# Differential attention and a gated feed-forward on one core: the second exponentials' scaling moved from two engines to ScalarE alone, with corrected entries in the build-time plan

## The chip, the cores and the metric

The kernel runs on one core of a Trainium2 chip. The metric is the device time of one execution in microseconds (us). The core has five engines that work through their own instruction lists in order and wait on semaphores: TensorE (PE in the profile, PEld for its weight loads), VectorE (DVE), ScalarE (ACT), GpSimd (POOL), and SyncE (SP), which here only issues transfers.

## The reference

The input is 2048 tokens of 256 values. The reference is a differential attention with 16 query heads and 8 key heads of width 128, and then a gated feed-forward, each with a layer norm before and behind it and a residual.

```python
def attn_map(qi, ki):
    s = jnp.einsum('bqhd,bkhd->bhqk', qi, ki) * scale
    s = jnp.where(causal, s, neg)
    return jax.nn.softmax(s, axis=-1)
p1 = attn_map(q[:, :, :, 0], k[:, :, :, 0])
p2 = attn_map(q[:, :, :, 1], k[:, :, :, 1])
lam = lam1 - lam2 + LAMBDA_INIT
p = p1 - lam * p2
o = jnp.einsum('bhqk,bkhe->bqhe', p, v)
rms = jax.lax.rsqrt(jnp.mean(o * o, axis=-1, keepdims=True) + EPS)
o = o * rms * subln_w * (1.0 - LAMBDA_INIT)
return o.reshape(B, S, H * D) @ out_w.T + out_b
...
x = fwht(x * SU_ug) / SCALE
x = jax.nn.silu(x @ W_gate.T * ws_gate) * (x @ W_up.T * ws_up)
x = fwht(x * SU_dp) / SCALE
x = x @ W_down.T * ws_down
```

## The kernel before

**Tiling.** The attention is cut into 4 groups of heads, a group into 16 *duos*, a duo into two blocks of 128 query rows that together see 17 key blocks. A duo `d` has 5 chunks `j` of 128 to 512 keys. So there are 64 duos and 320 chunks. For each chunk the score matrix is made twice, `m = 0` and `m = 1` (640 score chunks).

**One chunk's way.** PE makes the scores in one of four score banks (lines 1038, 1041 and 1044). DVE takes the maximum (1441, with the mask 1436, negated by 1445). ACT takes the exponential and its row sum (step `E`, line 1211), which frees the score bank; `m = 0` goes to a ring named e1, `m = 1` to a ring named e2 (both are called `e_all` in the rows). When both maps of a block are done, DVE works out `ratio` (1733: minus lambda times the one sum over the other) and `gain` (1736). Then e2 is multiplied by `ratio` (step `E2`: by ACT in line 1226 or by POOL in line 1782), POOL adds it to e1 (step `MIX`, line 1749), ACT writes the high half of the product with `gain` as 16-bit numbers (step `SPLIT`, line 1233), DVE the low half (line 1452), SP issues a transposing transfer, and PE multiplies the result by the values (step `PV`, lines 1065 to 1067). The output of a block is then normed (ACT 1241, DVE 1708, POOL 1756, ACT 1249, DVE 1482), transposed and multiplied by the output weights (step `OP`, 1118).

**Around it.** Query projections (step `QP`, PE 1137, ACT 1267, DVE 1494) run two blocks of tokens ahead. In the last group the weights of the feed-forward are prepared between the chunks: POOL builds a Hadamard matrix (`HAD`) and eight sums or differences of weight halves (`FB`, line 1859), ACT and DVE split each (`FH`, 1334 and 1616), PE multiplies by the matrix (`F`), and ACT (1352) and DVE (1624) move the product out of its bank. Of the four weight loads for that, two are issued behind `FB` 1 and 3, and `FB` 4 to 7 read them.

**What sets the order.** `plan()` runs when the kernel is built. It steps through time with a recorded duration for every operation, starts on each engine the ready head with the lowest rank (then the oldest), and so writes out five fixed lists, one for each engine. The hardware then follows these lists; a step whose input is late holds up all that stands behind it in its list. `E` has rank 1, `MIX` and `SPLIT` rank 2, `E2` on ACT rank 3. In `start`, POOL may take a `MIX` whose `E2` nobody has begun, and then does the `E2` itself just ahead of it; an `E2` that POOL has taken is dropped from ACT's line.

Of the kernel before, what the change touches and what calls it, by code (L numbers as in the profile page):

```python
# [173 lines left out]
def plan():  # L174
# [5 lines left out]
    waiting, ending, now, count = {}, [], [0.0], [0]  # L180
    scaling, mixed = set(), set()
    free_at = {e: 0.0 for e in ("PE", "ACT", "DVE", "POOL", "SP")}
# [12 lines left out]
    def spawn(kind, what):  # L195
        pe = ("PE", kind, what)
        if kind == "S":
# [4 lines left out]
            if last:  # L202
                own = [jj for jj, ch in enumerate(duo_chunks(d)) if ch[0] == o]
                for jj in own:
                    qq, ww = CHUNKS * d + jj, duo_chunks(d)[jj][4]
                    room = [("DVE", "SPLIT", duo_of(x)) for x in e1_blockers[qq]] if m == 0 else \
                        [("SP", "SPLIT", duo_of(x)) for x in e2_blockers[qq]]
                    add("E", "ACT", "E", (d, m, jj), 0.23 + 0.00084 * ww, [("DVE", "S", what)] + room, 1)
                if m == 1:
                    add("I", "DVE", "SUMS", o, 0.1, [("ACT", "E", (d, 1, own[-1]))], 0)  # L210
                    add("I", "DVE", "INV", o, 0.08, [("DVE", "SUMS", o)], 0)
                    add("I", "DVE", "GAIN", o, 0.16, [("DVE", "INV", o)] + ([] if o else [("DVE", "LAM2", None)]), 0)
                    for jj in own:
                        qq, ww = CHUNKS * d + jj, duo_chunks(d)[jj][4]
                        room = [("PE", "PV", duo_of(x)) for x in pt_blockers[qq]]
                        add("A", "ACT", "E2", (d, jj), 0.19 + 0.00083 * ww, [("DVE", "GAIN", o)], 3)
                        add("M", "POOL", "MIX", (d, jj), 0.19 + 0.00212 * ww, [("DVE", "GAIN", o)], 2)
                        add("H", "ACT", "SPLIT", (d, jj), 0.19 + 0.00083 * ww, [("POOL", "MIX", (d, jj))], 2)
                        add("L", "DVE", "SPLIT", (d, jj), 0.13 + 0.00115 * ww, [("ACT", "SPLIT", (d, jj))], 2)
                        add("T", "SP", "SPLIT", (d, jj), 0.3 + 0.002 * ww, [("DVE", "SPLIT", (d, jj))] + room, 0, 2.2)  # L220
        elif kind == "PV":
            o, last = duo_chunks(what[0])[what[1]][0], duo_chunks(what[0])[what[1]][5]
            if last:
                add("P", "ACT", "SQ", o, 0.40, [pe] + ([("DVE", "VE", o - 4)] if o >= 4 else []), 0)
                add("N", "DVE", "VE", o, 0.08, [("ACT", "SQ", o)], 0)
                add("N", "POOL", "OT", o, 0.55, [("DVE", "VE", o)] + ([("DVE", "OL", o - 4)] if o >= 4 else []), 0)
                add("R", "ACT", "OH", o, 0.29, [("POOL", "OT", o)] + ([("SP", "OX", o - 4)] if o >= 4 else []), 0)
                add("R", "DVE", "OL", o, 0.4, [("ACT", "OH", o)], 0)
                add("X", "SP", "OX", o, 1.2, [("DVE", "OL", o)] + ([("PE", "OP", o - 4)] if o >= 4 else []), 0, 2.2)
# [266 lines left out]
    def start(engine):  # L496
        for line in (waiting.get(("ACT", "A"), ()),):
            while line and line[0][1].what in mixed:
                line.popleft()
        heads = [line[0] for (e, _), line in waiting.items() if e == engine and line]  # L500
        heads = [(op.rank, n, op) for n, op in heads if all(x in done for x in op.after)
                 and not (op.kind == "MIX" and op.what in scaling and ("ACT", "E2", op.what) not in done)]
        if not heads:
# [5 lines left out]
        us = op.us  # L509
        if op.kind == "E2":  # L510
            scaling.add(op.what)
# [82 lines left out]
def build(nc, hidden, w_qkv, w_o, cols, rows, lams, w_ug, w_d, out):  # L594
# [10 lines left out]
    with ExitStack() as whole:  # L605
# [18 lines left out]
        with ExitStack() as att:  # L624
# [128 lines left out]
            def h_tile(c, jt, lo, tt):  # L753
# [34 lines left out]
             s_full, s_act, s_dve, t_full, t_hi, t_lo, r_full, r_hi, r_free, kv_full, kv_act, kv_dve, v_lo,  # L788
             neg_ready, sums_ready, ratio_step, ratio_ready, gain_ready, e2_scaled, e2_act, p_pool, p_hi, p_lo, pv_done, o_hi, o_lo,
             msq_ready, rms_step, rms_ready) = semaphores(  # L790
# [83 lines left out]
            def e2_of(q, w):  # L874
                return e2_all[:, e2_places[q]:e2_places[q] + w]
# [320 lines left out]
            def _(act):  # L1196
# [543 lines left out]
            def _(pool):  # L1740
                def mix(d, j):
                    o, s, _, _, w, _ = duo_chunks(d)[j]
                    q = CHUNKS * d + j
                    a, b = e1_of(q, w), e2_of(q, w)
                    if (d, j) in scaled_by_act:
                        pool.wait_ge(e2_act, scaled_by_act[d, j] + 1)
                    else:
                        pool.wait_ge(e2_scaled, scaled_by_pool[d, j] + 1)
                    pool.tensor_tensor(a, a, b, ALU.add).then_inc(p_pool, 1)  # L1749
# [224 lines left out]
```

## Time and profile before

| | |
|---|---|
| median of 3 runs | 1285.94 us (1284.38 to 1286.74) |
| profiled execution, its own time | 1285.75 us |
| its span, first to last instruction | 1283.5 us |
| mean granted TensorE clock | 0.985 |
| busy: PE, DVE, ACT, POOL | 1210.5, 1066.1, 995.4, 700.8 us |
| `E2` on ACT (line 1226) | 197 times, 121.5 us |
| `E2` on POOL (line 1782) | 123 times, 89.6 us |
| `MIX` on POOL (line 1749) | 320 times, 372.9 us |

The attention fills the span from about 60 us to about 1130 us; behind it only the feed-forward runs. Matmuls overlap in the records, so PE's busy time is time in which at least one is under way. Two neighbouring instructions of ACT or DVE overlap a little in the same way.

### The profile page before, as it was taken

Reading aid. Unit: us, or ns where it says so; the run is one execution under the profiler, and the core shown is the slowest. Engines: PE = TensorE matmul, PEld = TensorE weight load, DVE = VectorE, ACT = ScalarE, POOL = GpSimd, SP = SyncE. Lnnn points to the kernel's source line nnn. Section 1 sums busy time; section 2 is a strip of 40 time slices with the busy share of each in tenths; the row PEclk is TensorE's granted clock in tenths of the full one; section 3 lists DMA queues with packets and bytes.
Section 4 is the critical chain, followed back from the end, with each engine's and each line's share of the span. In section 5 each row is a group of like instructions: output and inputs, shape, how many; then the busy total and the mean of one; then the engine's idle time right before and its main releaser. Section 6 shows DMA issues by size and latency. Waiting matters only on the chain.

```text
span 1283.5 us, 26516 instructions
## 1 busy us (share of the span) xinstructions
PE 1210.5 (94%) x8102; PEld 1018.7 (79%) x8102; DVE 1066.1 (83%) x2876; ACT 995.4 (78%) x2599; POOL 700.8 (55%) x797
## 2 busy tenths in 40 slices
PE   8899999999999999999999999999988797898998
PEld 7787887877888878888878788788876685786887
DVE  6889999888789998989799989888889899637545
ACT  5788888889688888978789889887877788745341
POOL 3464645454655655536565655445588574556532
PEclk9899999999999999999999999999998899999999
DMA  3145545564265554532555455445543453720001
GB/s 128 57 76 105 88 85 89 102 101 71 50 127 90 99 91 89 103 70 55 126 97 95 85 94 102 74 75 114 100 85 76 93 90 69 143 46 1 29 17 37
DMA packets 368154, 106.62 MB, mean 83 GB/s; under 512 B 359312, under 2 KB 365712, under 8 KB 367504
## 3 DMA queue, kind: packets, MB, share of 16 engines
q1 hardware_dynamic: 366672, 103.37, 42.6%
q8 instruction: 67, 1.10, 0.4%
q10 hardware_dynamic: 1344, 1.57, 0.3%
q14 instruction: 71, 0.58, 0.1%
HBM read 14.71 MB, written 2.10 MB: 13 GB/s over the span
## 4 chain that ended last, share of the span: by engine, by line
PE 47%; DVE 29%; issue 8%; ACT 8%; POOL 4%; DMA 4%; SPq 1%; ACTq 0%; DVEq 0%; POOLq 0%
DVE p L1452 7%; PE score_bank L1172 7%; DVE mx L1441 6%; PE score_bank L1038 5%; PE score_bank L1044 4%; PE score_bank L1041 4%; ACT e_all L1211 4%; DVE score_bank L1436 4%; PE turn_bank L1065 2%; POOL e_all L1749 2%; PE turn_bank L1066 2%; PE turn_bank L1067 2%; DMA p16T<-p 2%; PE proj_bank L1065 2%; PE proj_bank L1067 2%
## 5 line engine op out<-in xcount | busy, mean ns | idle before, releaser
L1749 POOL TENSOR_TENSOR e_all<-e_all 128x512 f32<-128x512 f32 (+3 forms) x320 | 372.9, 1179 | 141.9 <-ACT e_all L1226 131.6
L1211 ACT ACTIVATE e_all<-score_bank,negmx 128x512 f32<-128x512 f32 (+2 forms) x640 | 394.1, 625 | 60.8 <-DVE negmx L1445 46.3
L1038 PE MATMUL score_bank<-k_hi,q_hi 128*128 128x512 f32 (+2 forms) x640 | 257.1, 402 | 32.9 <-ACT e_all L1211 16.9
L1452 DVE SCALAR_TENSOR_TENSOR p<-e_all,gain,p 128x512 f16<-128x512 f32 (+3 forms) x320 | 266.2, 846 | 9.3 <-ACT p L1233 8.9
L1441 DVE TENSOR_REDUCE mx<-score_bank 128x1 f32<-128x512 f32 (+1 forms) x384 | 242.5, 636 | 18.3 <-PE score_bank L1044 17.4
L1041 PE MATMUL score_bank<-k_lo,q_hi 128*128 128x512 f32 (+2 forms) x640 | 233.0, 364 | 0.4 <-DVE k_lo L1502 0.4
L1044 PE MATMUL score_bank<-k_hi,q_lo 128*128 128x512 f32 (+2 forms) x640 | 233.1, 364 | 0.0
L1233 ACT ACTIVATE p<-e_all,gain 128x512 f16<-128x512 f32 (+3 forms) x320 | 203.9, 665 | 13.0 <-POOL e_all L1749 12.6
L1038 PEld LDWEIGHTS score_bank<-k_hi,q_hi 128*128 128x128 f32 x640 | 121.7, 190 | 75.6 <-ACT e_all L1211 33.6
L1782 POOL TENSOR_SCALAR e_all<-e_all,ratio 128x512 f32<-128x512 f32 (+3 forms) x123 | 89.6, 728 | 156.8 <-DVE ratio L1733 155.9
L1756 POOL TENSOR_TENSOR few<-few,half_neg 128x1 f32<-128x1 f32 x128 | 78.5, 614 | 142.0 <-DVE few L1708 141.8
L1065 PE MATMUL turn_bank<-v,p16T 128*128 128x256 f16 x553 | 152.4, 276 | 3.7 <-DVE q_lo L1494 1.7
L1066 PE MATMUL turn_bank<-v,p16T 128*128 128x256 f16 x553 | 151.6, 274 | 0.0
L1067 PE MATMUL turn_bank<-v,p16T 128*128 128x256 f16 x553 | 151.5, 274 | 0.0
L1226 ACT ACTIVATE e_all<-e_all,ratio 128x512 f32<-128x512 f32 (+2 forms) x197 | 121.5, 660 | 16.5 <-DVE ratio L1733 16.3
L1044 PEld LDWEIGHTS score_bank<-k_hi,q_lo 128*128 128x128 f32 x640 | 121.5, 190 | 14.0
L1211 ACT ACTIVATION_READ_ACCUMULATOR e_all<-score_bank,negmx 128x1 f32 x640 | 131.9, 206 | 0.0
L1041 PEld LDWEIGHTS score_bank<-k_lo,q_hi 128*128 128x128 f32 x640 | 122.3, 191 | 7.0 <-DVE k_lo L1502 0.6
L1436 DVE CUSTOM_DVE_ANT_0 score_bank<-score_bank,mask 128x384 f32<-128x384 f32 (+2 forms) x192 | 110.7, 577 | 14.7 <-PE score_bank L1044 14.3
L1065 PE MATMUL proj_bank<-v,p16T 128*128 128x256 f16 x326 | 89.4, 274 | 0.0
L1067 PE MATMUL proj_bank<-v,p16T 128*128 128x256 f16 x326 | 89.0, 273 | 0.0
L1066 PE MATMUL proj_bank<-v,p16T 128*128 128x256 f16 x326 | 89.0, 273 | 0.0
(393 smaller groups left out, 2738.6 us busy)
## 6 DMA issues: line engine op xcount, KB each, us to landing
p16T<-p SPq DMA_TRANSPOSE x320, 3.1
w_raw<-in_w_qkv_dram SPq DMA_DIRECT2D x3, 1024.0 KB, 5.3
w_raw<-in_w_o_dram SPq DMA_DIRECT2D x4, 512.0 KB, 3.3
oT<-o SPq DMA_TRANSPOSE x128, 2.5
bv<-in_hidden_dram SPq DMA_DIRECT2D x8, 256.0 KB, 2.9
w_raw<-in_w_ug_dram SPq DMA_DIRECT2D x4, 512.0 KB, 4.3
out_dram<-e SPq DMA_DIRECT2D x16, 128.0 KB, 1.7
e<-in_w_d_dram SPq DMA_DIRECT2D x1, 1024.0 KB, 5.9
```

The costliest lines, as they stand in the source:

```text
L1038: pe.matmul(bank[:, 0:w], qh, kh, start=True, stop=False)
L1041: pe.matmul(bank[:, 0:w], qh, kl, start=False, stop=False)
L1044: pe.matmul(bank[:, 0:w], ql, kh, start=False, stop=True).then_inc(s_full, 1)
L1065: pe.matmul(bank[:, 0:HID], hi, v16[:, kt, 0, :], start=(kt == 0), stop=False)
L1066: pe.matmul(bank[:, 0:HID], hi, v16[:, kt, 1, :], start=False, stop=False)
L1067: mm = pe.matmul(bank[:, 0:HID], lo, v16[:, kt, 0, :], start=False, stop=(kt == i))
L1211: act.activation(e, S[k % NS][:, 0:w], ACT.Exp, bias=negmx[:, d % 2, m, s:s + 1], scale=-1.0 if alone else 1.0, accum_out=ssum[:, d % 4, s ...
L1233: act.activation(halves_of(q, w)[0], e1_of(q, w), ACT.Copy, scale=gain[:, d % 4, s:s + 1]).then_inc(p_hi, 1)
L1436: dve.tensor_tensor_reduce(out=S[k % NS][:, 0:w], in0=S[k % NS][:, 0:w], in1=mask[:, BANK - w:], scale=1.0, scalar=LOWEST, op0=ALU.add, op ...
L1441: dve.tensor_reduce(mx[:, d % 2, m, s, c:c + 1], S[k % NS][:, 0:w], X, ALU.max)\
L1452: dve.scalar_tensor_tensor(out=halves_of(q, w)[1], in0=e1_of(q, w), scalar=gain[:, d % 4, s:s + 1], in1=halves_of(q, w)[0], op0=ALU.mult, ...
L1749: pool.tensor_tensor(a, a, b, ALU.add).then_inc(p_pool, 1)
```

## The change

All 320 `E2` are ACT's, with rank 2 instead of 3; in the plan a `MIX` waits for its `E2`; POOL's form of it, and the two sets by which the engines shared them, are gone. POOL's wait is now for ACT's count of `E2`, which are done in the order of the chunks. Some recorded durations of the plan are changed: `GAIN` 0.16 to 0.26, DVE's `SPLIT` 0.00115 to 0.00104 a column, `SQ` 0.40 to 0.37, `VE` 0.08 to 0.13, `OH` 0.29 to 0.37. The plan also learns that the two late weight loads take 5.0 and that `FB` 4 to 7 wait for them. No instruction but `E2` changes its engine or its form.

```diff
-                    add("I", "DVE", "GAIN", o, 0.16, [("DVE", "INV", o)] + ([] if o else [("DVE", "LAM2", None)]), 0)
+                    add("I", "DVE", "GAIN", o, 0.26, [("DVE", "INV", o)] + ([] if o else [("DVE", "LAM2", None)]), 0)
...
-                        add("A", "ACT", "E2", (d, jj), 0.19 + 0.00083 * ww, [("DVE", "GAIN", o)], 3)
-                        add("M", "POOL", "MIX", (d, jj), 0.19 + 0.00212 * ww, [("DVE", "GAIN", o)], 2)
+                        add("A", "ACT", "E2", (d, jj), 0.19 + 0.00083 * ww, [("DVE", "GAIN", o)], 2)
+                        add("M", "POOL", "MIX", (d, jj), 0.19 + 0.00212 * ww, [("ACT", "E2", (d, jj))], 2)
...
-                        add("L", "DVE", "SPLIT", (d, jj), 0.13 + 0.00115 * ww, [("ACT", "SPLIT", (d, jj))], 2)
+                        add("L", "DVE", "SPLIT", (d, jj), 0.13 + 0.00104 * ww, [("ACT", "SPLIT", (d, jj))], 2)
...
-            add("FB", "POOL", kind, what, 1.35, [("POOL", "HAD", None)] + ([("DVE", "FH", what - 2)] if what > 1 else []), 3)
-            add("D", "SP", kind, what, 0.3, [("POOL", kind, what)], 1)
+            loaded = [("SP", "FB", what // 2 * 2 - 3)] if what >= 4 else []
+            add("FB", "POOL", kind, what, 1.35, [("POOL", "HAD", None)] + ([("DVE", "FH", what - 2)] if what > 1 else []) + loaded, 3)
+            add("D", "SP", kind, what, 0.3, [("POOL", kind, what)], 1, 5.0 if what in (1, 3) else 0.0)
...
-        if op.kind == "MIX":
-            mixed.add(op.what)
-            if op.what not in scaling:
-                orders[engine].insert(-1, ("E2", op.what))
-                us += 0.32 + 0.00085 * duo_chunks(op.what[0])[op.what[1]][4]
...
-                        act.activation(e, e, ACT.Copy, scale=ratio[:, d % 4, s:s + 1]).then_inc(e2_act, 1)
+                        act.activation(e, e, ACT.Copy, scale=ratio[:, d % 4, s:s + 1]).then_inc(e2_scaled, 1)
...
-                    if kind == "E2":
-                        d, j = what
-                        o, s, _, _, w, _ = duo_chunks(d)[j]
-                        e = e2_of(CHUNKS * d + j, w)
-                        pool.wait_ge(ratio_ready, o + 1)
-                        pool.tensor_scalar(e, e, ratio[:, d % 4, s:s + 1], 0.0, ALU.mult, ALU.add).then_inc(e2_scaled, 1)
```

The lists that the plan writes differ in many places. Three of them follow. The line numbers of the changed kernel are lower by 14 on DVE and ACT in these parts (1212 is 1226, 1610 is 1624) and by 17 to 23 on POOL (1732 is 1749, 1836 is 1859).

ACT in the second group, around duo 21, in the kernel before:

```order
L1233 ACTIVATE p_78<-e_all,gain 128x512
L1226 ACTIVATE e_all<-e_all,ratio 128x384
L1233 ACTIVATE p_78<-e_all,gain 128x384
L1226 ACTIVATE e_all<-e_all,ratio 128x384
L1211 ACTIVATE e_all,ssum<-score_bank,negmx 128x512
L1211 ACTIVATE e_all,ssum<-score_bank,negmx 128x384 x2
L1233 ACTIVATE p_78<-e_all,gain 128x384 x2
L1211 ACTIVATE e_all,ssum<-score_bank,negmx 128x512
```

and in the changed kernel:

```order
L1219 ACTIVATE p_78<-e_all,gain 128x512
L1212 ACTIVATE e_all<-e_all,ratio 128x512
L1212 ACTIVATE e_all<-e_all,ratio 128x384
L1253 ACTIVATE q_hi<-turn_bank,bq 128x256
L1197 ACTIVATE e_all,ssum<-score_bank,negmx 128x512
L1197 ACTIVATE e_all,ssum<-score_bank,negmx 128x384
L1219 ACTIVATE p_78<-e_all,gain 128x512
L1219 ACTIVATE p_78<-e_all,gain 128x384
L1212 ACTIVATE e_all<-e_all,ratio 128x384
L1197 ACTIVATE e_all,ssum<-score_bank,negmx 128x512
```

Scalings (1212) now stand two in a row here, ahead of the exponentials (1197) and of a query projection (1253).

POOL in the last group, between the sums of weights `FB` 4, 5 and `FB` 6, 7, in the kernel before:

```order
L1859 TENSOR_TENSOR v_sum<-w_raw 128x512 x2
L1782 TENSOR_SCALAR e_all<-e_all,ratio 128x512
L1749 TENSOR_TENSOR e_all<-e_all 128x512 x2
L1782 TENSOR_SCALAR e_all<-e_all,ratio 128x384
L1749 TENSOR_TENSOR e_all<-e_all 128x384
L1782 TENSOR_SCALAR e_all<-e_all,ratio 128x384
L1749 TENSOR_TENSOR e_all<-e_all 128x384
L1782 TENSOR_SCALAR e_all<-e_all,ratio 128x384
L1749 TENSOR_TENSOR e_all<-e_all 128x384
L1782 TENSOR_SCALAR e_all<-e_all,ratio 128x256
L1749 TENSOR_TENSOR e_all<-e_all 128x256
L1782 TENSOR_SCALAR e_all<-e_all,ratio 128x512
```

(two more scalings and three more sums of 512 follow ahead of `FB` 6), and in the changed kernel:

```order
L1836 TENSOR_TENSOR v_sum<-w_raw 128x512 x2
L1732 TENSOR_TENSOR e_all<-e_all 128x384
L1732 TENSOR_TENSOR e_all<-e_all 128x512 x2
L1732 TENSOR_TENSOR e_all<-e_all 128x384 x2
L1836 TENSOR_TENSOR v_sum<-w_raw 128x512 x2
```

The scalings are gone, and five sums (1732) instead of nine stand between the two pairs.

DVE a little later, up to the first of two steps that take the product of the folds `F` 2 and 3 out of its bank (1624), in the kernel before:

```order
L1441 TENSOR_REDUCE mx<-score_bank 128x1
L1452 SCALAR_TENSOR_TENSOR p_78<-e_all,gain,p_78 128x384 x2
L1452 SCALAR_TENSOR_TENSOR p_78<-e_all,gain,p_78 128x256
L1452 SCALAR_TENSOR_TENSOR p_78<-e_all,gain,p_78 128x512 x2
L1718 TENSOR_REDUCE s_97<-ssum 128x2
L1708 TENSOR_SCALAR few<-few 128x1
L1452 SCALAR_TENSOR_TENSOR p_78<-e_all,gain,p_78 128x512
L1723 RECIPROCAL inv<-s_97 128x2
L1624 SCALAR_TENSOR_TENSOR spare<-turn_bank,su_s,spare 128x512
```

and in the changed kernel:

```order
L1427 TENSOR_REDUCE mx<-score_bank 128x1
L1438 SCALAR_TENSOR_TENSOR p_78<-e_all,gain,p_78 128x384
L1438 SCALAR_TENSOR_TENSOR p_78<-e_all,gain,p_78 128x256
L1468 SCALAR_TENSOR_TENSOR o_64<-turn_bank,few,o_64 128x256
L1704 TENSOR_REDUCE s_97<-ssum 128x2
L1709 RECIPROCAL inv<-s_97 128x2
L1719 SCALAR_TENSOR_TENSOR ratio<-s_97,inv,neg_lam 128x1
L1722 TENSOR_SCALAR gain<-inv,few 128x1
L1438 SCALAR_TENSOR_TENSOR p_78<-e_all,gain,p_78 128x512
L1610 SCALAR_TENSOR_TENSOR spare<-sum_bank,su_s,spare 128x512
```

Three low halves (1438) instead of six stand between the last maximum and that step.

## Rows read from the trace of the kernel before

**Rows 1.** The page: busy time by engine; the chain that ended last, by engine
```profile
PE 1210.5 (94%) x8102; PEld 1018.7 (79%) x8102; DVE 1066.1 (83%) x2876; ACT 995.4 (78%) x2599; POOL 700.8 (55%) x797
...
PE 47%; DVE 29%; issue 8%; ACT 8%; POOL 4%; DMA 4%; SPq 1%; ACTq 0%; DVEq 0%; POOLq 0%
```

**Rows 2.** Busy time by stretch: PE, PEld, DVE, ACT, POOL; granted clock, DMA share
```profile
60.00:1080.00 1020.00, 971.12 (x6772) 818.74 (x6771) 906.53 (x2466) 865.21 (x2319) 583.40 (x647) 0.99 0.49 90
840.00:1080.00 240.00, 214.28 (x1466) 180.64 (x1464) 212.84 (x572) 197.80 (x523) 156.10 (x182) 0.96 0.46 89
```

**Rows 3.** The first of these stretches, POOL's line 1782 alone
```profile
60.00:1080.00 1020.00, 84.86 (x117) 0.99 0.49 90
```

**Rows 4.** Groups by form, ACT's line 1226: busy us, mean ns, idle before
```profile
L1226 ACT ACTIVATE e_all<-e_all,ratio 128x512 f32<-128x512 f32 x98 | 67.5, 721 | 13.2 <-DVE ratio L1733 13.1
...
L1226 ACT ACTIVATE e_all<-e_all,ratio 128x384 f32<-128x384 f32 x89 | 52.0, 614 | 3.0 <-DVE ratio L1733 2.9
...
L1226 ACT ACTIVATE e_all<-e_all,ratio 128x256 f32<-128x256 f32 x7 | 3.5, 503 | 0.3 <-DVE ratio L1733 0.2
```

**Rows 5.** Groups by form, POOL's line 1782
```profile
L1782 POOL TENSOR_SCALAR e_all<-e_all,ratio 128x512 f32<-128x512 f32 x62 | 48.0, 774 | 100.2 <-DVE ratio L1733 99.6
...
L1782 POOL TENSOR_SCALAR e_all<-e_all,ratio 128x384 f32<-128x384 f32 x47 | 33.7, 716 | 39.7 <-DVE ratio L1733 39.5
```

**Rows 6.** The waits: who waited for whom, us in total, times, longest
```profile
POOL e_all L1782 <- DVE ratio L1733: 155.9, 65, 10.2
...
POOL e_all L1749 <- ACT e_all L1226: 131.6, 52, 10.2
...
PEld score_bank L1038 <- ACT e_all L1211: 33.6, 60, 2.9
...
ACT o L1249 <- POOL few L1756: 26.3, 39, 3.8
...
ACT p L1233 <- POOL e_all L1749: 12.6, 27, 1.0
```

**Rows 7.** Busy time in a slice of 16 us
```profile
512.00:528.00 16.00, 15.97 (x120) 13.81 (x119) 15.68 (x39) 15.78 (x43) 9.91 (x12) 1.00 0.42 95
```

**Rows 8.** The same slice, POOL's line 1782 alone
```profile
512.00:528.00 16.00, 1.69 (x3) 1.00 0.42 95
```

**Rows 9.** POOL's timeline near 378 us: start, duration
```profile
377.74 0.69 POOL L1782 TENSOR_SCALAR e_all<-e_all,ratio 128x512 f32<-128x512 f32 x1
```

**Rows 10.** DVE's timeline at the same moment
```profile
377.98 0.99 DVE L1452 SCALAR_TENSOR_TENSOR p<-e_all,gain,p 128x512 f16<-128x512 f32 x1 [0.97 <-ACT p L1233]
```

**Rows 11.** DVE's line 1452: duration min/median/max in ns, all forms
```profile
L1452 DVE SCALAR_TENSOR_TENSOR p<-e_all,gain,p x320: 342/741/1829, 60.0 to 1124.0; 128x512 f16<-128x512 f32 x80, 128x384 f16<-128x384 f32 x68, 128x256 f16<-128x256 f32 x8, 128x128 f16<-128x128 f32 x4
```

**Rows 12.** PE's timeline at 1002 us, with the idle time before it
```profile
1002.36 0.80 PE L1137 MATMUL turn_bank<-xT_hi,wq_hi 128*128 128x256 f32 x2 [6.89 <-DVE spare L1624]
```

**Rows 13.** DVE's timeline from 995 to 1002 us
```profile
995.39 5.35 DVE L1452 SCALAR_TENSOR_TENSOR p<-e_all,gain,p 128x384 f16<-128x384 f32 x5
...
1001.59 0.72 DVE L1624 SCALAR_TENSOR_TENSOR spare<-turn_bank,su_s,spare 128x512 fp32r<-128x512 f32 x1
```

**Rows 14.** The slice around it: busy time and granted clock
```profile
992.00:1008.00 16.00, 9.11 (x48) 7.53 (x46) 14.58 (x29) 7.99 (x20) 11.55 (x13) 0.68 0.28 54
```

**Rows 15.** The chain at and behind it: start, us, what
```profile
1002.36 1.65 PE turn_bank L1137 x6
...
1007.66 0.21 PE proj_bank L1067
1007.88 0.11 PE proj_bank L1065
...
1011.72 0.71 PE turn_bank L1137 x6
```

**Rows 16.** POOL's line 1859 (the folds' sums), and its engine's idle time before it
```profile
L1859 POOL TENSOR_TENSOR v_sum<-w_raw x8: 1264/1294/1829, 950.7 to 997.6; 128x512 f32<-128x512 f32 x8
its engine sat idle before it (us, times) until:
```

More of the change, by code:

```diff
@@ L180, in plan @@
     waiting, ending, now, count = {}, [], [0.0], [0]
-    scaling, mixed = set(), set()
     free_at = {e: 0.0 for e in ("PE", "ACT", "DVE", "POOL", "SP")}
@@ L223, in spawn @@
             if last:
-                add("P", "ACT", "SQ", o, 0.40, [pe] + ([("DVE", "VE", o - 4)] if o >= 4 else []), 0)
-                add("N", "DVE", "VE", o, 0.08, [("ACT", "SQ", o)], 0)
+                add("P", "ACT", "SQ", o, 0.37, [pe] + ([("DVE", "VE", o - 4)] if o >= 4 else []), 0)
+                add("N", "DVE", "VE", o, 0.13, [("ACT", "SQ", o)], 0)
                 add("N", "POOL", "OT", o, 0.55, [("DVE", "VE", o)] + ([("DVE", "OL", o - 4)] if o >= 4 else []), 0)
-                add("R", "ACT", "OH", o, 0.29, [("POOL", "OT", o)] + ([("SP", "OX", o - 4)] if o >= 4 else []), 0)
+                add("R", "ACT", "OH", o, 0.37, [("POOL", "OT", o)] + ([("SP", "OX", o - 4)] if o >= 4 else []), 0)
                 add("R", "DVE", "OL", o, 0.4, [("ACT", "OH", o)], 0)
@@ L496, in start @@
     def start(engine):
-        for line in (waiting.get(("ACT", "A"), ()),):
-            while line and line[0][1].what in mixed:
-                line.popleft()
         heads = [line[0] for (e, _), line in waiting.items() if e == engine and line]
-        heads = [(op.rank, n, op) for n, op in heads if all(x in done for x in op.after)
-                 and not (op.kind == "MIX" and op.what in scaling and ("ACT", "E2", op.what) not in done)]
+        heads = [(op.rank, n, op) for n, op in heads if all(x in done for x in op.after)]
         if not heads:
@@ L509, in start @@
         us = op.us
-        if op.kind == "E2":
-            scaling.add(op.what)
-        if op.kind == "MIX":
-            mixed.add(op.what)
-            if op.what not in scaling:
-                orders[engine].insert(-1, ("E2", op.what))
-                us += 0.32 + 0.00085 * duo_chunks(op.what[0])[op.what[1]][4]
         free_at[engine] = now[0] + us
@@ L794, in build @@
                 "r_hi", "r_free", "kv_full", "kv_act", "kv_dve", "v_lo", "neg_ready", "sums_ready", "ratio_step",
-                "ratio_ready", "gain_ready", "e2_scaled", "e2_act", "p_pool", "p_hi", "p_lo", "pv_done", "o_hi", "o_lo", "msq_ready",
+                "ratio_ready", "gain_ready", "e2_scaled", "p_pool", "p_hi", "p_lo", "pv_done", "o_hi", "o_lo", "msq_ready",
                 "rms_step", "rms_ready")
@@ L844, in build @@
                             neg_use[o, m] = len(neg_use)
-            scaled_by_act = {x: n for n, x in enumerate([x for k, x in orders["ACT"] if k == "E2"])}
-            scaled_by_pool = {x: n for n, x in enumerate([x for k, x in orders["POOL"] if k == "E2"])}
             WORK = (T[0], T[1], R, O)
@@ L1744, in mix @@
                     a, b = e1_of(q, w), e2_of(q, w)
[L1745 to L1748, printed above, removed]
+                    pool.wait_ge(e2_scaled, q + 1)
                     pool.tensor_tensor(a, a, b, ALU.add).then_inc(p_pool, 1)
@@ L1776, in _ @@
                 for kind, what in orders["POOL"] + tail:
-                    if kind == "E2":
-                        d, j = what
-                        o, s, _, _, w, _ = duo_chunks(d)[j]
-                        e = e2_of(CHUNKS * d + j, w)
-                        pool.wait_ge(ratio_ready, o + 1)
-                        pool.tensor_scalar(e, e, ratio[:, d % 4, s:s + 1], 0.0, ALU.mult, ALU.add).then_inc(e2_scaled, 1)
-                    elif kind == "MIX":
+                    if kind == "MIX":
                         mix(*what)
```

2 lines of the change are left out of this document (1 added, 1 removed).

## The prediction

> **What bounds the kernel now.** I read the page first. PE has work under way for 94% of the span, DVE for 83%, ACT for 78%, POOL for 55%, and the chain that ended last runs 47% over PE, 29% over DVE and only 8% over ACT [rows 1]. The change touches the attention alone, so the busy time by stretch is the next view. From 60 to 1080 us PE is busy 971.1 of 1020 us (95%), DVE 906.5 (89%), ACT 865.2 (84.8%), POOL 583.4 (57%) [rows 2]. Three engines are close to full and feed each other in fixed lists: PE leads, but neither DVE nor ACT has much to give. The last part differs: from 840 to 1080 us PE is at 214.3 of 240 us (89%) and DVE at 212.8 (89%), with the clock at 0.96 [rows 2]. There PE is not the leader; the work on the feed-forward's weights makes DVE and POOL late.
>
> The waits say what an idle moment is worth. POOL waits 155.9 us for `ratio` ahead of its scalings and 131.6 us for ACT's scalings ahead of a sum [rows 6]. These are large and cost nothing, as ACT waits for POOL's sums only 12.6 us in all [rows 6]. The wait to watch is PE's: its weight loads for scores stand 33.6 us, 60 times, for an exponential of ACT that has to free the score bank [rows 6]. That is where more work on ACT comes back to the leader.
>
> **What is moved.** 123 scalings leave POOL, 62 of 512 columns and 47 of 384 at least [rows 5], the other 14 narrower. ACT's own scalings take 721, 614 and 503 ns by width [rows 4]. So ACT gains 62 x 0.721 + 47 x 0.614 + 14 x 0.50 = 44.7 + 28.9 + 7.0 = 81 us (a little high, since some of the 14 are of 128 columns). POOL loses its 89.6 us. In the stretch of 1020 us lie 117 of the 123 [rows 3], so ACT gains 77 us there.
>
> **Term 1, ACT's queue.** ACT's share rises from 865/1020 = 0.848 to 942/1020 = 0.924. Its idle time there falls from 155 to 78 us: there is room for the work, but half of the slack is gone. How much PE feels can't be read from a row, so I bound it. From below it is nothing: in the plan an exponential has rank 1 and a scaling rank 2, so a scaling goes where the plan sees no exponential ready. From above I let PE's wait for exponentials grow as busy over idle share does, from 0.848/0.152 = 5.6 to 0.924/0.076 = 12.2, a factor of 2.2, which adds 33.6 x 1.2 = 40 us. The truth is nearer to the lower end, because the lists keep the ranks, but not at it, because the chip doesn't keep the plan's times, and a scaling just ahead of an exponential then holds it for up to 0.7 us. The listing of ACT around duo 21 shows such a pair. I take a third: +13 us.
>
> **Term 2, where ACT is already full.** In the slice from 512 to 528 us ACT is busy 15.78 of 16 us [rows 7], and POOL scales for 1.69 us there, three times [rows 8]. At ACT's durations, about the same, that doesn't fit into the 0.22 us left: +1.5 us. I take +2 for this slice and others that come near it. Bounds: 0, if the new lists shift the work, and 5, if there are several such slices.
>
> **Term 3, DVE beside POOL.** One of POOL's scalings runs from 377.74 us for 0.69 us [rows 9]. DVE's low half of 512 columns begins 0.24 us later and takes 0.99 us [rows 10], against a median of 0.741 us over all widths, to which the undisturbed 512 comes close [rows 11]. So it is held for about 0.25 us. POOL scales for 84.9 of 1020 us, 8.3% of the time [rows 3]; 8.3% of 320 low halves are 27, times 0.25 us = 7 us of DVE. DVE is 29% of the chain [rows 1]: -2 us. Bounds: 0 (the lists now put POOL's sums closer together, and a low half can meet a sum instead, with up to 1.829 us [rows 11]) and -7. The Trainium skill, page "SBUF — State Buffer", section "SBUF: two separate sides", has the rule that VectorE with two SBUF inputs and GpSimd take the shared pair as an exclusive lock, and that whoever starts first keeps it for the whole instruction. The trace agrees in kind; the row's 0.25 us is short of the 0.45 us that the scaling still had to run. By the rule with a mean remainder of 0.35 us the term would be -3 instead of -2 us.
>
> **Term 4, POOL's room.** POOL's busy share falls from 57% to 49%. ACT waits 26.3 us for POOL's step of the norm and 12.6 us for its sums [rows 6]. If these shrink with the share, by 15%, ACT saves 6 us of waits, and with ACT at 8% of the chain [rows 1] that is under 1 us; I take -1, bounds 0 and -6. Against it stands that all 320 sums now wait for ACT, not 197; a later sum delays a product, and PE has a queue of those.
>
> **Term 5, the hole in the last group.** At 1002.36 us PE resumes after 6.89 us without work [rows 12]. It waited for DVE to empty a bank of the folds, and DVE had five low halves in 5.35 us in front of that and one more behind them [rows 13]. Each of them takes about 1.07 us, as POOL's sums run beside them. The clock in that slice is 0.68 of its mean [rows 14], that is, part of it at 1.2 instead of 2.4 GHz, granted after PE stood still. The six matmuls behind the hole take 1.65 us, and the same six 0.71 us nine us later; a matmul with the values still takes 0.21 us at 1007.66 and 0.11 us from 1007.88 on [rows 15]. So the 5.5 us from 1002.36 on run at about half speed and lose 2.7 us, and the whole hole costs 9.6 us. The new lists have three low halves instead of six ahead of that step, no scalings on POOL and five sums instead of nine before it. I take that this halves the 6.9 us and keeps the clock's loss in part: -4 us. Bounds: 0 (another hole opens elsewhere, since every list is new) and -9.6.
>
> **Edits at nothing.** The new durations of `GAIN`, `SQ`, `VE`, `OH` and `SPLIT` and the loads change no instruction, only the lists; their worth is in term 5 and in the range. The loads in particular: POOL never stood idle ahead of line 1859 [rows 16], so neither load was late, and entering them removes no wait.
>
> **Sum.** 13 + 2 - 2 - 1 - 4 = +8 us. On the profiled execution's own 1285.75 us this is 1293.8 us; the median of the runs lies 0.2 us higher, at 1285.94, so 1294 us.
>
> **The rivals.** 0.2% (2.6 us) is about what a measurement of this kernel can tell from no change, so "same" is 1283.4 to 1288.5 us.
> - *Forecast: ACT's queue reaches PE in part.* 1289 to 1304 us. Chance 0.51.
> - *ACT becomes the leader.* If scalings stand in front of exponentials whenever a bank is awaited, term 1 goes to its upper end: 1286 + 40 + 5 - 7 = 1324 us, and 1305 is passed at two thirds of term 1. It decides when ACT's busy share passes 0.95 in the stretch of 1020 us. Against it: 78 us of idle time are left, and 8% of the chain is little to start from. Chance 0.09.
> - *ACT hides all of it.* Terms 1 and 2 near 3, the gains as above: 1286 + 3 - 7 = 1282, or 1286 if the hole stays. For it: the ranks, and 155 us of idle time. This gives "same" for the most part. Chance 0.16.
> - *The other side: the last group's POOL is the real limit.* There POOL and DVE make PE late; and if the hole closes in full (-9.6), DVE gains its bound (-7, on the path as it is), and ACT's queue costs no more than 5, the time is 1286 - 9.6 - 7 + 5 = 1274 us, and 1278 with half of DVE's gain. It decides where the hole's 9.6 us go, and needs term 1 under 9. For it: DVE is at 89% and ACT at 197.8/240 = 82% from 840 to 1080 us [rows 2], so ACT has more room there than anywhere. Against it: PE is at 95% in the whole stretch, where POOL is not late. Chance 0.24.
> - The change does what it says: the lists have no scaling on POOL left, so nothing is kept for that case.
>
> Slower by over 0.2%: 0.51 + 0.09 = 0.60. Within: 0.16, less what falls under 1283.4 and more from the others' edges, 0.15. Faster: 0.25. The range: below 1277 us I leave half of the last rival's end (0.08), above 1306 the second rival (0.09). So 1277 to 1306 us; the forecast's own is 1289 to 1304.
>
> **What the profile would show.** Right: line 1212 (the old 1226) 320 times with some 200 us; ACT near 1075 us, POOL near 611 us; ACT busy 92% from 60 to 1080 us; PE's wait for an exponential at scores at 45 to 50 us instead of 33.6; DVE's low halves at 255 to 262 us instead of 266; a gap of 3 to 4 us or none where PE waits for the folds. Term 1 is wrong if that wait is under 36 or over 60 us; term 3 if the low halves take as long as before; term 5 if a gap of 6 us or more with a low clock is still there, or a new one. The whole is wrong if ACT's waits for DVE, not its load, decide, or if the new lists alone move the time by more than the load does.

## The result, and the profile after

The changed kernel takes 1294.27 us (median of 9 runs, 1287.94 to 1301.61), the kernel before 1286.06 us in its 9. The ratio is 1.0069 with a 95% interval of 1.0049 to 1.0088: slower by 9 us. The profiled execution has a span of 1294.6 us. Its runs spread over 14 us, those of the kernel before over 6 us.

The page of the changed kernel, busy time by engine and the chain by engine, against [rows 1]:

```profile
PE 1212.2 (94%) x8102; PEld 1015.4 (78%) x8102; DVE 1062.2 (82%) x2876; ACT 1049.6 (81%) x2722; POOL 607.9 (47%) x674
...
PE 48%; DVE 24%; ACT 11%; issue 9%; POOL 4%; DMA 4%; SPq 1%; ACTq 0%; POOLq 0%; DVEq 0%
```

ACT's busy time rises by 54 us, from 995.4 to 1049.6, POOL's falls by 93 us. ACT's share of the chain goes from 8% to 11%, DVE's from 29% to 24%. The stretches of [rows 2]:

```profile
60.00:1080.00 1020.00, 962.71 (x6691) 808.82 (x6691) 885.46 (x2415) 896.01 (x2377) 484.51 (x521) 0.99 0.50 88
840.00:1080.00 240.00, 215.95 (x1484) 180.68 (x1483) 203.86 (x553) 203.72 (x528) 130.58 (x147) 0.97 0.47 86
```

In the same 1020 us PE gets 962.7 us of work under way instead of 971.1, ACT is busy 87.8% instead of 84.8%. From 840 to 1080 us PE has 1.7 us more than before, so the loss lies ahead of 840 us, before the feed-forward's weights are prepared. ACT's scalings in the kernel before and in the changed one (the old line 1226 is 1212), the widest form of the latter, then the waits (against [rows 6]):

```profile
L1226 ACT ACTIVATE e_all<-e_all,ratio 128x512 f32<-128x512 f32 (+2 forms) x197 | 121.5, 660 | 16.5 <-DVE ratio L1733 16.3
...
L1212 ACT ACTIVATE e_all<-e_all,ratio 128x512 f32<-128x512 f32 (+3 forms) x320 | 197.2, 667 | 13.4 <-DVE ratio L1719 13.3
...
L1212 ACT ACTIVATE e_all<-e_all,ratio 128x512 f32<-128x512 f32 x160 | 111.1, 731 | 10.6 <-DVE ratio L1719 10.5
```

```profile
POOL e_all L1732 <- ACT e_all L1212: 336.4, 137, 8.5
...
PEld score_bank L1024 <- issue: 30.7, 54, 2.9
...
PEld score_bank L1024 <- ACT e_all L1197: 28.0, 59, 1.9
...
ACT o L1235 <- POOL few L1739: 17.2, 22, 2.0
...
ACT p L1219 <- POOL e_all L1732: 8.9, 15, 1.8
```

Count times mean gives the single durations: 320 x 0.667 = 213 us now, 197 x 0.660 = 130 us before. POOL's waits for ACT's scalings grew from 131.6 to 336.4 us, which by itself says nothing of their price. PE's wait for exponentials, the row that the prediction watched, did not grow: 28.0 us instead of 33.6. Each kernel has one more row for the same weight loads, in which no releaser could be named; that of the kernel before is

```profile
PEld score_bank L1038 <- issue: 26.3, 48, 2.8
```

Both rows together are 59.9 us before and 58.7 us after. ACT waits less for POOL: 17.2 instead of 26.3 us for the norm, 8.9 instead of 12.6 us for the sums.

What grew is seen at PE's own matmuls. In the kernel before, a product with the values begins with line 1065, an output product with line 1118. The number behind the second bar is the time that PE stood idle just ahead of them:

```profile
L1065 PE MATMUL turn_bank<-v,p16T 128*128 128x256 f16 x553 | 152.4, 276 | 3.7 <-DVE q_lo L1494 1.7 <-DMA p16T<-p 0.9 <-DVE k_lo L1502 0.6
...
L1118 PE MATMUL sum_bank<-wo,oT 128*128 128x256 f16 x210 | 28.9, 274 | 6.0 <-DMA oT<-o 6.0
```

and in the changed kernel (1051 and 1104):

```profile
L1051 PE MATMUL turn_bank<-v,p16T 128*128 128x256 f16 x557 | 153.8, 276 | 4.8 <-DMA p16T<-p 3.2 <-DVE q_lo L1480 0.8 <-DVE k_lo L1488 0.7
...
L1051 PE MATMUL sum_bank<-v,p16T 128*128 128x256 f16 x273 | 76.1, 279 | 4.6 <-DVE xT_lo L1626 2.7 <-DVE acc L1520 1.9
...
L1051 PE MATMUL proj_bank<-v,p16T 128*128 128x256 f16 x258 | 70.6, 274 | 2.9 <-DVE acc L1520 2.1 <-DMA p16T<-p 0.5 <-issue 0.2
...
L1104 PE MATMUL proj_bank<-wo,oT 128*128 128x256 f16 x198 | 27.8, 278 | 6.8 <-DMA oT<-o 6.8
```

Over all banks, PE's idle time ahead of the products with the values rose from 3.7 to 12.3 us, and ahead of the output products from 7.1 to 11.7 us. Ahead of scores it fell from 32.9 to 30.0 us. All of PE's idle time, its span less its busy time, rose by 9.4 us.

DVE's low halves, from the page's groups, against 266.2 us before:

```profile
L1438 DVE SCALAR_TENSOR_TENSOR p<-e_all,gain,p 128x512 f16<-128x512 f32 (+3 forms) x320 | 260.3, 828 | 10.1 <-ACT p L1219 9.8
```

### The profile page after: what moved, and what is told of

Read it like the earlier page. It is cut to its first block, busy times and chain, and to the rows that moved or that the text cites. A ratio compares the mean times of both kernels' runs of the same rounds, so it can differ in the third digit from the quotient of the medians.

```text
span 1294.6 us, 26516 instructions
## 1 busy us (share of the span) xinstructions
PE 1212.2 (94%) x8102; PEld 1015.4 (78%) x8102; DVE 1062.2 (82%) x2876; ACT 1049.6 (81%) x2722; POOL 607.9 (47%) x674
## 4 chain that ended last, share of the span: by engine, by line
PE 48%; DVE 24%; ACT 11%; issue 9%; POOL 4%; DMA 4%; SPq 1%; ACTq 0%; POOLq 0%; DVEq 0%
DVE p L1438 6%; PE score_bank L1158 6%; PE score_bank L1024 6%; PE score_bank L1030 5%; PE score_bank L1027 5%; ACT e_all L1197 5%; DVE mx L1427 4%; DVE score_bank L1422 3%; PE turn_bank L1051 2%; PE turn_bank L1052 2%; PE turn_bank L1053 2%; POOL e_all L1732 2%; ACT e_all L1212 2%; DMA p16T<-p 2%; PE turn_bank L1104 2%
## 5 line engine op out<-in xcount | busy, mean ns | idle before, releaser
L1732 POOL TENSOR_TENSOR e_all<-e_all 128x512 f32<-128x512 f32 (+3 forms) x320 | 370.8, 1177 | 336.8 <-ACT e_all L1212 336.4
L1438 DVE SCALAR_TENSOR_TENSOR p<-e_all,gain,p 128x512 f16<-128x512 f32 (+3 forms) x320 | 260.3, 828 | 10.1 <-ACT p L1219 9.8
L1212 ACT ACTIVATE e_all<-e_all,ratio 128x512 f32<-128x512 f32 (+3 forms) x320 | 197.2, 667 | 13.4 <-DVE ratio L1719 13.3
L1739 POOL TENSOR_TENSOR few<-few,half_neg 128x1 f32<-128x1 f32 x128 | 73.7, 578 | 197.0 <-DVE few L1694 196.8
L1197 ACT ACTIVATION_READ_ACCUMULATOR e_all<-score_bank,negmx 128x1 f32 x640 | 136.4, 213 | 0.0
L1051 PE MATMUL sum_bank<-v,p16T 128*128 128x256 f16 x273 | 76.1, 279 | 4.6 <-DVE xT_lo L1626 2.7
L1053 PE MATMUL sum_bank<-v,p16T 128*128 128x256 f16 x273 | 75.8, 278 | 0.0
L1052 PE MATMUL sum_bank<-v,p16T 128*128 128x256 f16 x273 | 75.8, 278 | 0.0
L1051 PEld LDWEIGHTS turn_bank<-v,p16T 128*128 128x128 f16 x557 | 54.9, 98 | 25.1 <-issue 13.3
```

The costliest lines, as they stand in the source:

```text
L1051: pe.matmul(bank[:, 0:HID], hi, v16[:, kt, 0, :], start=(kt == 0), stop=False)
L1052: pe.matmul(bank[:, 0:HID], hi, v16[:, kt, 1, :], start=False, stop=False)
L1053: mm = pe.matmul(bank[:, 0:HID], lo, v16[:, kt, 0, :], start=False, stop=(kt == i))
L1197: act.activation(e, S[k % NS][:, 0:w], ACT.Exp, bias=negmx[:, d % 2, m, s:s + 1], scale=-1.0 if alone else 1.0, accum_out=ssum[:, d % 4, s ...
L1438: dve.scalar_tensor_tensor(out=halves_of(q, w)[1], in0=e1_of(q, w), scalar=gain[:, d % 4, s:s + 1], in1=halves_of(q, w)[0], op0=ALU.mult, ...
```

## The experiments

All ratios are to the kernel before on the same chip, with their 95% intervals.

**Which part of the change costs.** e1 takes the code of the change and the old table:

```diff
-                    add("I", "DVE", "GAIN", o, 0.26, ...
+                    add("I", "DVE", "GAIN", o, 0.16, ...
...
-            loaded = [("SP", "FB", what // 2 * 2 - 3)] if what >= 4 else []
```

(and the other four durations likewise). 

> All scalings on ScalarE as in the change, but the plan keeps its old durations and doesn't know the weight loads. Load theory (ScalarE's added 54 us of busy time make the change slower): as the changed kernel, ratio to before 1.005 to 1.009. Table theory (the new durations or the loads make worse lists): 1.000 to 1.002. Scatter theory (every new set of lists moves the time by several us, whatever it is): anywhere from 0.997 to 1.012, away from the changed kernel's 1.007 as easily as on it.

Measured: 1289.18 us, ratio 1.0040 (1.0024 to 1.0055).

e2 is the reverse, the kernel before with all entries of the new table:

```diff
-                    add("I", "DVE", "GAIN", o, 0.16, ...
+                    add("I", "DVE", "GAIN", o, 0.26, ...
...
+            loaded = [("SP", "FB", what // 2 * 2 - 3)] if what >= 4 else []
```

> The scalings shared by ScalarE and GpSimd as before, with the new durations and the two loads in the plan. Load theory: ratio 0.998 to 1.002. Table theory: 1.005 to 1.009. Scatter theory: anywhere from 0.995 to 1.008.

Measured: 1291.11 us, ratio 1.0047 (1.0031 to 1.0063). So each half alone is slower, by 5 and 6 us, and both together by 9. Neither the load theory nor the table theory had both; only the wide ranges of the scatter theory hold both. The two weight loads have no part in it: with and without them the plan writes the same five lists, entry for entry, in the kernel before and in the changed one. All of the table's effect is that of the five durations. The new `GAIN` and `OH` are nearer to what the profile records (`OH`, line 1249, takes 0.48 us there; the plan had 0.29 and now has 0.37), yet this set of lists was slower.

**Load or lists.** e3 keeps every list of the changed kernel and moves only the 123 scalings back to POOL:

```diff
+    for x in POOL_SCALES:
+        orders["ACT"].remove(("E2", x))
+        orders["POOL"].insert(orders["POOL"].index(("MIX", x)), ("E2", x))
```

> All lists of the changed kernel, but the 123 scalings that GpSimd did before are taken out of ScalarE's list and put in GpSimd's, each just ahead of its sum. Every other instruction keeps its place. Load theory: the loss goes, ratio to before 0.998 to 1.002. Scatter or table theory (the lists, not the load): it stays at 1.005 to 1.009. If GpSimd's relief had been worth something, it may even be slower than the changed kernel.

Measured: 1302.94 us, ratio 1.0141 (1.0116 to 1.0167). The work that ACT got rid of did not bring the time back; it went up by another 9 us. The chain by engine and one wait of e3:

```profile
PE 43%; DVE 26%; issue 9%; POOL 9%; ACT 8%; DMA 4%; SPq 1%; ACTq 0%; POOLq 0%; DVEq 0%
```

```profile
ACT p L1240 <- POOL e_all L1756: 22.9, 30, 1.7
```

POOL's share of the chain is 9%, against 4% both before and after, and ACT waits 22.9 us for POOL's sums, against 8.9 us in the changed kernel. But the profiled execution of e3 took 1296.45 us, 6.5 us less than the median and as much as that of the changed kernel (1296.41 us). So these rows tell where e3 differs, and not where its 9 us go.

e4 is the mirror image, the lists of the kernel before with the 123 scalings in ACT's list:

```diff
+    for kind, x in [entry for entry in orders["POOL"] if entry[0] == "E2"]:
+        orders["POOL"].remove((kind, x))
+        at = next((n for n, (k, w) in enumerate(orders["ACT"])
+                   if ("ACT", k, w) in began and began["ACT", k, w] >= began["POOL", "MIX", x]), None)
+        orders["ACT"].insert(len(orders["ACT"]) if at is None else at, (kind, x))
```

> All lists of the kernel before, but GpSimd's 123 scalings are put in ScalarE's list, where the plan had GpSimd begin the sum; every other instruction keeps its place. Load theory: ratio 1.006 or more (these places were never planned for ScalarE, so up to 1.015). Lists theory: 0.998 to 1.002.

Measured: 1304.07 us, ratio 1.0151 (1.0129 to 1.0174), at the top of what the load theory expected. The chain and PE's waits for score banks in e4:

```profile
PE 42%; DVE 21%; ACT 17%; issue 11%; DMA 4%; POOL 3%; SPq 1%; ACTq 0%; POOLq 0%; DVEq 0%
```

```profile
PEld score_bank L1044 <- issue: 42.6, 73, 3.1
...
PEld score_bank L1044 <- ACT e_all L1217: 41.0, 74, 2.9
```

ACT is 17% of the chain, and the two rows sum to 83.6 us, against 59.9 us before: 24 us more, 7 of them in the row that names the exponentials and 16 in the row without a releaser. That fits the mechanism of the prediction's term 1. It is there when nobody plans for the extra load, and absent (58.7 us) when the plan does. Both crossed kernels are slower than either original, so lists and share can't be judged apart: lists made for one share do badly with the other.

**The price of each engine's time, with the lists held.** e5 is the changed kernel, but ACT scales only 32 columns in those 123 scalings (most of these second exponentials stay unscaled):

```diff
+                        if what in POOL_SCALES:
+                            e = e[:, 0:32]
                         act.activation(e, e, ACT.Copy, scale=ratio[:, d % 4, s:s + 1]).then_inc(e2_scaled, 1)
```

> The changed kernel with all its lists; of the 123 scalings that GpSimd did before, ScalarE now scales only the first 32 columns, so that the rest of these second exponentials stays unscaled and the output is another. That takes about 45 us of work out of ScalarE and puts none elsewhere. Load theory: the ratio to before falls to 1.000 or below (down to 0.997). Lists theory: it stays at 1.004 to 1.008. Run e3 gave 1.014 with the same 123 off ScalarE's list but on GpSimd's: if this run is near 1.000, the two scalings' place on GpSimd cost e3 its time; if it is at 1.014 as well, the lists do.

Measured: 1289.56 us, ratio 1.0039 (1.0016 to 1.0061). The page's group of all scalings in e5, and the narrow form alone:

```profile
L1228 ACT ACTIVATE e_all<-e_all,ratio 128x512 f32<-128x512 f32 (+3 forms) x320 | 155.9, 535 | 16.8 <-DVE ratio L1735 16.4
```

```profile
L1228 ACT ACTIVATE e_all<-e_all,ratio 128x32 f32<-128x32 f32 x123 | 38.1, 329 | 6.3 <-DVE ratio L1735 6.0
```

The scalings' busy time fell from 197.2 to 155.9 us, ACT's whole busy time from 1049.6 to 1016.3 us. So 41 us less of scalings, or 33 us of ACT, gave back 0.0030 of the ratio, some 4 us. The intervals of the two ratios overlap, and the gain lies between 0 and 8 us. As an estimate, a microsecond of ACT's busy time is worth about 0.1 us here. The run fits neither theory's range: the load theory wanted 1.000 or less, the lists theory 1.004 to 1.008.

The runs e3 and e5 have the same lists but for these 123 scalings. Short ones on ACT (e5) and whole ones on POOL (e3) are 13 us apart, so whole scalings on POOL are dear in the changed kernel's lists too.

e6 does the same to POOL's 123 scalings in the kernel before:

```diff
+                        e = e[:, 0:32]
                         pool.tensor_scalar(e, e, ratio[:, d % 4, s:s + 1], 0.0, ALU.mult, ALU.add).then_inc(e2_scaled, 1)
```

> The kernel before with all its lists; GpSimd scales only the first 32 columns in its 123 scalings, so the rest stays unscaled and the output is another. About 60 us of work leave GpSimd. If GpSimd's room is worth what the prediction took (terms 3 and 4, 3 us), the ratio is 0.996 to 0.999. If GpSimd's lateness was the real limit of the kernel before, 0.985 to 0.993. If nothing of it reaches TensorE, 0.999 to 1.001.

Measured: 1273.61 us, ratio 0.9914 (0.9893 to 0.9935): 11 us faster (8 to 14), in the range named for GpSimd's lateness as the real limit. POOL's scalings of e6, the stretch of the attention, and three waits:

```profile
L1783 POOL TENSOR_SCALAR e_all<-e_all,ratio 128x32 f32<-128x32 f32 x123 | 47.3, 385 | 165.4 <-DVE ratio L1733 164.6
```

```profile
60.00:1080.00 1020.00, 976.10 (x6815) 823.38 (x6813) 906.38 (x2483) 870.76 (x2333) 544.55 (x650) 0.99 0.50 90
```

```profile
PEld score_bank L1038 <- ACT e_all L1211: 29.6, 56, 2.5
...
ACT o L1249 <- POOL few L1756: 20.4, 32, 3.3
...
ACT p L1233 <- POOL e_all L1749: 6.3, 15, 0.9
```

42 us less on an engine that is busy 55% of the span gave 11 us, 0.26 us for each. The profiled execution took 1278.56 us, 5 us more than the median, so the rows hold some 7 of the 11 us. PE has 976.1 us under way instead of 971.1. PE's wait for exponentials fell by 4.0 us; ACT's two waits for POOL fell by 12.2 us together (5.9 for the norm, 6.3 for the sums), which is about the whole gain. DVE's total busy time fell from 1066.1 to 1057.3 us. This experiment gives the sum of these effects. It doesn't divide it into the shorter way from a softmax to its product, ACT's waits and the freer DVE. The shorter way alone is not enough as a reason: e5 shortens the same 123 scalings by as much (731 to 329 ns on ACT, 774 to 385 ns on POOL for the widest) and gave 4 us, though in other lists.

**How much is the draw of a list.** A meaningless edit of one recorded duration changes over a thousand places in the lists. Where the scalings are shared it also changes how: POOL gets 116 to 136 of them in these lists, not always 123. Three such edits were made in both kernels:

```diff
-                add("R", "DVE", "OL", o, 0.4, [("ACT", "OH", o)], 0)
+                add("R", "DVE", "OL", o, 0.42, [("ACT", "OH", o)], 0)
```

(e7 and e8), QP on VectorE 0.4 to 0.42 (e9 and e10), and

```diff
-                    add("E", "ACT", "E", (d, m, jj), 0.23 + 0.00084 * ww, [("DVE", "S", what)] + room, 1)
+                    add("E", "ACT", "E", (d, m, jj), 0.235 + 0.00084 * ww, [("DVE", "S", what)] + room, 1)
```

(e11 and e12).

> The kernel before with one meaningless edit in the plan: the low half of an output (OL on VectorE) is recorded with 0.42 instead of 0.40. Sharing and work are as before, the lists differ in over a thousand places. Scatter theory: the ratio lies anywhere from 0.994 to 1.008, typically 3 us or more from 1. If lists hardly matter: 0.999 to 1.001.

> The changed kernel with the same meaningless edit (OL 0.42 instead of 0.40). Load theory with scatter on top: 1.002 to 1.012, and above the run e7. Scatter alone: as e7, on either side of it.

> The kernel before with another meaningless edit in the plan (VectorE's QP 0.42 instead of 0.40): new lists, same sharing. Scatter theory, with the kernel before a lucky draw of its kind: 1.001 to 1.007, as e2 (1.0047) and e7 (1.0037). If the kernel before is an ordinary draw: 0.997 to 1.003.

> The changed kernel with the same edit (QP 0.42). Scatter theory with no cost of the sharing: as e9, on either side. Load theory: above e9 by 0.002 or more. Range 1.001 to 1.010.

> The kernel before with a third meaningless edit (an exponential recorded 0.005 longer). As e9: 1.001 to 1.007 if the kernel before is a lucky draw, 0.997 to 1.003 if not.

> The changed kernel with that third edit. As e10. Over the five lists of each sharing (before, e2, e7, e9, e11 against after, e1, e8, e10, e12) the load theory expects the means apart by 0.004 or more, the scatter theory by under 0.002.

| table | scalings shared | all on ACT |
|---|---|---|
| old | kernel before: 1 | e1: 1.0040 (1.0024 to 1.0055) |
| new | e2: 1.0047 (1.0031 to 1.0063) | changed kernel: 1.0069 (1.0049 to 1.0088) |
| OL edit | e7: 1.0037 (1.0024 to 1.0050) | e8: 1.0045 (1.0029 to 1.0062) |
| QP edit | e9: 1.0009 (0.9997 to 1.0020) | e10: 1.0046 (1.0029 to 1.0062) |
| E edit | e11: 0.9982 (0.9968 to 0.9995) | e12: 1.0102 (1.0086 to 1.0119) |

(The edits of the left column are on the old table, those of the right on the new one.) Five lists of each sharing have means of 1.0015 and 1.0060 and standard deviations of 0.0027 and 0.0026. The difference of the means is 0.0045, and with five lists on a side its 95% interval is 0.0007 to 0.0084. So both rival theories were partly right: lists of one kind scatter by 0.3% (a standard deviation of 3.4 us), moving all scalings to ACT at rank 2 costs 0.45% (6 us) on top, and every list with all scalings on ACT was slower than the kernel before. The load theory wanted 0.004 or more and the scatter theory under 0.002; the mean is in the load theory's range, but the interval reaches below 0.002. e11 is faster than the kernel before, by 0.18%, through a table edit of 0.005.

**Where the 6 us stand.** PE's idle time just ahead of its matmuls, in the one profiled execution of each of the ten kernels (us, mean of five, lowest and highest):

| PE idle ahead of | scalings shared | all on ACT |
|---|---|---|
| scores | 35.0 (31.8 to 41.2) | 28.5 (21.8 to 31.7) |
| products with the values | 5.4 (2.6 to 8.5) | 11.2 (6.0 to 15.3) |
| output products | 8.2 (3.9 to 11.2) | 12.0 (11.4 to 14.0) |
| query projections | 8.4 (5.4 to 10.2) | 9.4 (5.2 to 19.2) |
| all matmuls | 72.6 (68.3 to 77.5) | 77.5 (75.2 to 82.4) |

With all scalings on ACT, PE waits less for scores and more behind them, for the values' products and the outputs.

**What was not run.** The change also moves `E2` on ACT from rank 3 to rank 2, and no run separates the rank from the share. The time at which `plan()` itself ends says that it may matter. It ends at 1099.4 us for the kernel before and at 1112.5 us for the changed one. Over the five tables of each kind it ends at 1099.4 to 1102.8 us where scalings are shared and at 1107.0 to 1119.2 us where they are not, and the means are 13 us apart. With all scalings on ACT but at rank 3 the same five tables end at 1095.6 to 1109.8 us, 8 us earlier in the mean. So the plan foresees the direction, and puts more than half of its loss down to the rank. On the chip this isn't shown.

## Why the prediction was right

The direction and the sum were right: +8 us forecast, +9 measured (0.69% of 1286). That the sum came so near is luck. By the prediction's own signs terms 1 and 5 were wrong, term 4 was far off, and some errors cancelled. It also named as a sign against the whole that new lists alone could move the time by more than the load does: e2 moved it by 6 us through the table alone, as much as the move to ACT costs in the mean.

**The amount moved.** The 81 us were single durations, and as such right: 213 us for 320 scalings less 130 for 197 is 83. On the engine it is 54 us of busy time, as neighbours overlap. ACT ended at 87.8% of the stretch, not at 92.4%, also because 21 of the 54 us now lie behind 1080 us. This step was over-sized by half.

**Term 1 (+13 us, ACT's queue in front of the exponentials).** The mechanism fits e4, with 24 us more in these two rows. In the changed kernel it did not act, as 59.9 us became 58.7. The step that failed is the third of the upper bound that I took on the ground that the chip doesn't keep the plan's times. With lists planned for the load, none of it came at this place. The size of ACT's direct price is estimated from e5: some 4 us for 33 us of busy time, so about 6 for 54, with 0 to 12 open. What grew stands elsewhere, ahead of the products with the values (3.7 to 12.3 us) and the output products (7.1 to 11.7 us). The prediction named that way (a later sum delays a product) only as an objection in term 4, without a price. That it is ACT's later scalings which delay them is argued; the rows name late transfers and DVE's `acc` there.

**Term 2 (+2 us, full slices).** Not separately measurable. It is inside e5's price.

**Term 3 (-2 us, DVE beside POOL).** The low halves fell from 266.2 to 260.3 us, inside the 255 to 262 that were named. That is no proof of the term, since e3, with POOL's scalings back in the changed kernel's lists, has them as short:

```profile
L1459 DVE SCALAR_TENSOR_TENSOR p<-e_all,gain,p 128x512 f16<-128x512 f32 (+3 forms) x320 | 259.5, 825 | 10.0 <-ACT p L1240 9.6
```

Over the five lists of each kind the means are 264.4 and 263.7 us, between 259.9 and 267.3. In the old lists the relief is seen: e4 has 256.4 us and e6 260.7. So a low half can be held by a scaling, as [rows 10] show, but the 6 us of the changed kernel can as well be the draw of its list.

**Term 4 (-1 us, POOL's room).** The waits moved as forecast, 26.3 to 17.2 and 12.6 to 8.9 us. In the kernel before the value was far off. e6 gives 11 us for less than half of POOL's scaling time, where terms 3 and 4 had 3 us for all. In e6 the same two waits of ACT fell by 12.2 us, so the error was not in who waits but in multiplying by ACT's 8% of the chain. In the changed kernel they fell by 12.8 us, and no such gain is left: it is offset by what else the change does.

**Term 5 (-4 us, the hole).** Wrong. The hole is still there and nearly as long. PE's timeline, ACT's and DVE's just ahead of it, and the slice around:

```profile
1015.87 0.80 PE L1123 MATMUL sum_bank<-xT_hi,wq_hi 128*128 128x256 f32 x2 [6.44 <-DVE spare L1610]
```

```profile
1011.26 0.72 ACT L1212 ACTIVATE e_all<-e_all,ratio 128x512 f32<-128x512 f32 x1
1011.88 0.57 ACT L1197 ACTIVATE e_all<-score_bank,negmx 128x384 f32<-128x384 f32 x1
1012.34 0.20 ACT L1197 ACTIVATION_READ_ACCUMULATOR e_all<-score_bank,negmx 128x1 f32 x1
1012.43 1.33 ACT L1212 ACTIVATE e_all<-e_all,ratio 128x512 f32<-128x512 f32 x2
1013.66 0.71 ACT L1219 ACTIVATE p<-e_all,gain 128x512 f16<-128x512 f32 x1
1014.27 0.67 ACT L1338 ACTIVATE spare<-sum_bank,su_s 128x512 fp32r<-128x512 f32 x1
```

```profile
1014.40 0.75 DVE L1438 SCALAR_TENSOR_TENSOR p<-e_all,gain,p 128x512 f16<-128x512 f32 x1 [0.94 <-ACT p L1219]
1015.07 0.74 DVE L1610 SCALAR_TENSOR_TENSOR spare<-sum_bank,su_s,spare 128x512 fp32r<-128x512 f32 x1
```

```profile
1004.00:1020.00 16.00, 9.55 (x48) 7.83 (x47) 13.32 (x33) 15.18 (x36) 9.33 (x9) 0.82 0.38 70
```

PE stood for 6.44 us, against 6.89 us in [rows 12]. The granted clock of the slice is 0.82, and matmuls behind the hole run at the slower level as before: one of 512 columns took 0.63 us at 1018.17 us and 0.40 us at 1024.51 us. But the owner of the hole has changed. Before, ACT's half of this fold was done early,

```profile
990.13 0.69 ACT L1352 ACTIVATE spare<-turn_bank,su_s 128x512 fp32r<-128x512 f32 x1
```

and DVE was late with six low halves [rows 13]. Now DVE waits for ACT, 0.61 us ahead of 1012.57 us for an exponential and 0.94 us ahead of 1014.40 us for a high half, and the list of ACT has three scalings, an exponential and a high half between 1011.26 us and its half of the fold at 1014.27 us, with ACT busy 15.18 of 16 us. The prediction counted DVE's rows and not ACT's. In e12 the same wait is 2.4 us:

```profile
PEld sum_bank L1123 <- DVE spare L1610: 2.4, 1, 2.4
```

yet e12 is the slowest of its kind. The hole is one place among many and doesn't rank the lists.

**The edits at nothing.** The loads were rightly put at nothing. The durations were not worth nothing: in the kernel before they cost 6 us (e2), which is 1.2 standard deviations above the mean of its kind, and so within the scatter of lists. The size of a redrawn list, 3.4 us either way, is what the prediction's sum lacked. Its range of 1277 to 1306 us had room for it, for other reasons. The rank of `E2` has no term in it either.

**The sum as it stands now.** Of the 9 us, 6 are the move of all scalings to ACT at rank 2 (interval 1 to 11), and the rest lies within the scatter of lists: the changed kernel is 0.0009 above the mean of its kind, the kernel before 0.0015 below the mean of its own. How the 6 us come about is shown only in part. With the lists held, POOL's scalings cost 11 us or more in the kernel before (e6), and ACT's added scalings some 6 in the changed kernel (e5). In the old lists ACT's are far dearer: from short scalings on POOL (e6) to whole ones on ACT (e4) it is 30 us. These prices don't add up, since each was measured in other lists. The relief of POOL's 11 us does not show in the sum, so the new lists give it away somewhere; PE's idle time points at the values' and the output products, and the plan's own end at the rank. No run isolates either, so this stays open.

## What to carry to other kernels

Where a planner writes fixed lists, compare not one list with one list but several of each kind: a meaningless edit of a recorded duration is enough to make another, and here the lists of one kind scatter by 0.3%, about half of the effect that was sought. Look at the time at which the planner itself ends, too, and change a rank in a run of its own. Price an engine's time by shrinking its work with the lists held, and not by its busy share: 42 us of scalings on the engine that was busy 55% were worth 11 us (8 to 14), 41 us on one busy 81% were worth 4 (0 to 8), each in its own lists. One corrected table doesn't tell whether recorded durations nearer to the trace make better lists.

## What the runs showed of the hardware

ACT's single durations overstate its occupancy. Scalings of 512 columns last 731 ns each, but 123 more scalings with 83 us of durations added 54 us of busy time (29 us over 123, 0.24 us for each). In the timeline an instruction of ACT begins about 0.1 us before the recorded end of the one ahead of it: that at 1011.88 us follows one of 0.72 us from 1011.26 us.

A scaling has a high fixed part: of 32 columns it takes 329 ns on ACT and 385 ns on POOL, against 731 and 774 ns for 512 columns.
